# Two added waits on TensorE's own products in the expert stage of an attention and expert layer

## What is computed

```
x = L0_attn_x                                   # 4 x 1024 x 256
xn = _layernorm(x)
# attention of each batch of 1024 tokens
p = softmax(einsum('bqd,bkd->bqk', q, k) / 16); z = einsum('bqk,bkd->bqd', p, v)
# experts: 16 experts, the best 2 of each token, hidden width 128
h = silu(xt @ We_gate[e].T) * (xt @ We_up[e].T)
y = sum over the 2 chosen e of score * (h @ We_down[e].T)
# a shared expert of hidden width 512, gated by a sigmoid
return x + z + y + sigmoid(xt @ Wsg.T) * shared
```

## Time and profile before

| | |
|---|---|
| median of three executions | 540.95 us (540.4 to 541.15) |
| span of the profiled execution, first to last instruction | 535.7 us |
| median less span | 5.2 us |
| granted TensorE clock, mean | 0.997 of full speed |
| PE busy, share of the span | 96% (516.2 us) |
| VectorE, ScalarE, GpSimd busy | 75%, 52%, 32% |

### The profile page before, as it was taken

The page is one execution under the profiler, slowest core; times in us unless marked ns, Lnnn a source line. Parts: engine busy times, 40 slices in busy tenths (PEclk is TensorE's granted clock), DMA queues, the critical chain, the costliest instruction groups (busy, mean ns, idle before and its releaser), DMA issues.

```text
span 535.7 us, 10052 instructions
## 1 busy us (share of the span) xinstructions
PE 516.2 (96%) x3475; PEld 470.2 (88%) x3475; DVE 401.4 (75%) x842; ACT 277.7 (52%) x466; POOL 173.2 (32%) x161
## 2 busy tenths in 40 slices
PE   8999999999999699998999999999999999999997
PEld 6898898898888689988889989898989898989897
DVE  6997466898985466666666458998796969697986
ACT  4696865246652354444444545654453627272751
POOL 0001121101027565566662170517060424224302
PEclk9999999999999899999999999999999999999999
DMA  8926275122025355774456550443034111212112
GB/s 308 411 111 256 90 284 216 32 59 60 31 79 165 121 159 158 226 246 159 162 157 146 167 179 12 113 163 89 20 111 166 59 60 50 61 39 81 39 40 80
DMA packets 29840, 69.16 MB, mean 129 GB/s; under 512 B 4992, under 2 KB 9472, under 8 KB 28768
## 3 DMA queue, kind: packets, MB, share of 16 engines
q1 hardware_dynamic: 22496, 49.68, 25.8%
q0 software_dynamic: 6864, 18.75, 13.1%
q10 hardware_dynamic: 432, 0.09, 0.1%
HBM read 41.24 MB, written 27.26 MB: 128 GB/s over the span
## 4 chain that ended last, share of the span: by engine, by line
PE 81%; DVE 8%; issue 3%; another core or an unknown queue 3%; ACT 2%; DMA 1%; POOL 0%; SPq 0%; POOLq 0%; DVEq 0%; ACTq 0%
PE ps L771 52%; PE ps L981 9%; PE ps L777 6%; PE ps L911 6%; PE ps L1013 4%; PE ps L866 1%; ACT blk_xT L1105 1%; DVE blk_xT L1311 1%; PE ps L928 1%; DVE pT L1311 1%; DMA rows_y<-ytab,slot 1%; DVE probs_f L1646 1%; PE ps L875 1%; DVE place_hot L1497 1%
## 5 line engine op out<-in xcount | busy, mean ns | idle before, releaser
L758 POOL DMA_INDIRECT rows_y<-ytab,slot x64 | 77.6, 1213 | 148.1 <-DVE acc L1661 131.7
L738 POOL DMA_INDIRECT blk_x<-rows,row x79 | 81.0, 1025 | 79.4 <-DVE row L1512 30.5
L771 PE MATMUL ps<-vv,pT 128*128 128x258 f32 x768 | 97.6, 284 | 0.0
L771 PEld LDWEIGHTS ps<-vv,pT 128*128 128x128 f32 x768 | 95.2, 189 | 1.0
L771 PE MATMUL ps<-xT,shared_w 128*128 128x512 f32 x384 | 92.7, 394 | 0.4 <-DVE sil L1389 0.3
L771 PEld LDWEIGHTS ps<-xT,shared_w 128*128 128x128 f32 x384 | 70.7, 188 | 15.5 <-issue 0.9
L771 PE MATMUL ps<-qT,xbT_hi 128*128 128x512 f32 x256 | 79.3, 391 | 0.0
L981 PE MATMUL ps<-expert_w,blk_xT 128*128 x474 | 66.9, 290 | 5.8 <-DVE blk_xT L1311 5.3
L981 PEld LDWEIGHTS ps<-expert_w,blk_xT 128*128 128x128 f32 x474 | 59.5, 191 | 8.4 <-issue 8.3
L771 PEld LDWEIGHTS ps<-qT,xbT_hi 128*128 128x128 f32 x256 | 47.0, 188 | 9.2
L1299 ACT ACTIVATE probs_f<-probs_f 128x1024 f32<-128x1024 f32 x32 | 33.5, 1048 | 35.4 <-DVE probs_f L1646 35.4
(11 more groups left out here) (166 smaller groups left out, 857.7 us busy)
## 6 DMA issues: line engine op xcount, KB each, us to landing
ytab<-blk_y SPq DMA_DIRECT2D x40, 256.0 KB
keys<-xT SPq DMA_DIRECT2D x8, 1024.0 KB, 6.1
stage_e<-in_experts SPq DMA_DIRECT2D x16, 384.0 KB, 3.1
rows<-xn SPq DMA_DIRECT2D x8, 512.0 KB, 3.5
xbT_hi<-keys SPq DMA_DIRECT2D x8, 512.0 KB
xbT_lo<-keys SPq DMA_DIRECT2D x8, 512.0 KB
out<-acc SPq DMA_DIRECT2D x32, 128.0 KB
acc<-in_x SPq DMA_DIRECT2D x7, 512.0 KB, 9.0
```

Source lines behind the costliest of these rows:

```text
L738: e.indirect_dma_start(out=blk_x[:, q, n, :], out_offset=None, in_=rows, in_offset=bass.IndirectOffsetOnAxis(ap=row[:, 2 * b + n:2 * b + n ...
L758: e.indirect_dma_start(out=rows_y[:, r, k, :], out_offset=None, in_=ytab, in_offset=bass.IndirectOffsetOnAxis(ap=slot[:, k, i:i + 1], axis=0),
L771: ins = e.matmul(dst, stationary(p, k), moving(q, k), start=(n == 0), stop=(n == total - 1))
```

## The change

Two steps of TensorE's program get their waits in another order and one wait more each.

In `blk_hidden` the wait for the gated values was first in the code, and is now behind the wait for the buffer. A wait follows for `blk_gu` at `2 * (b + 1) + 1`: the first block of pair `b + 1`, whose twelve products stand directly ahead in TensorE's stream. In `blk_turn` the bank's wait now comes first and the wait for the fetched rows second, and from pair 4 on a wait follows for `blk_downed` at `2 * (b - 4) + 1`: the first block of pair `b - 4`, whose six products stand directly ahead. No other engine's program changes, and nothing is moved past another instruction.

```diff
                 elif kind == "blk_turn":
                     b, q = a[0], a[0] % XR
+                    bank = turn_bank(("blk_turn", b))
                     e.wait_ge(blk_loaded[q], 16 * (2 * (b // XR) + used(b)))
-                    bank = turn_bank(("blk_turn", b))
+                    if b >= 4:
+                        e.wait_ge(blk_downed, 2 * (b - 4) + 1)
                     turn(ps[:, bank, :], [blk_x[:, q, n, k * P:(k + 1) * P] for n in range(used(b)) for k in range(KD)],
                          blk_turned)
...
                     b, r = a[0], a[0] % 2
-                    e.wait_ge(blk_hidden, b + 1)
                     if b >= 2:
                         e.wait_ge(blk_hT_lo, b - 1)
                     else:
                         e.wait_ge(shared_added, 4 * NCH)
+                    e.wait_ge(blk_hidden, b + 1)
+                    if b + 1 < PAIRS:
+                        e.wait_ge(blk_gu, 2 * (b + 1) + 1)
                     turn(ps[:, 4 + r, :], [blk_h[:, r, n, :] for n in range(used(b))], blk_h_turned)
```

## The result

The changed kernel takes 554.25 us (median of four executions, 553.22 to 554.86), the kernel before beside it 540.68. The ratio is 1.025, interval 1.024 to 1.027: 2.5% slower. The forecast said slower, but only by 4.3 us, and its range ended at 550. The profiled execution has a span of 551.1 us, 15.4 more than before.

What follows compares the result with a forecast made beforehand. TensorE, busy 81% of the span, was taken as the bound, with late signals stalling the middle stretch. Eight gaps outside it (1.8 us) plus 2.5 us gave 4.3 us: 540.95 becomes 545.2 us, range 534 to 550.

Steps and rivals of the forecast that it cites:

- The reordered waits: Waits reordered in TensorE's `blk_hidden` and `blk_turn`: 0.01 us, only where `blk_hidden` or the rows are late; taken as 0.
- the wait for `blk_gu`: Ahead of the transposes of `blk_h`, 39 times: 0.40 us to spare, so 0 unless the signal is later than that.
- The gap of a TENSOR_LOAD: Ahead of every second product group, behind the `blk_downed` wait: 0.22 us each, 18 times, 4.0 us if all show.
- the term of the middle stretch: Experts' stage, 223.6 to 289.4 us: TensorE loses 1.2 us a cycle, 0.95 already lost; ten cycles cost 2.5 us.
- The 5.2 us that I took as lying around the span: Time outside the profiled span of 535.7 us, kept unchanged to go from span to measured time.
- 75 waits of 50 to 100 ns: 39 `blk_gu` and 36 `blk_downed` semaphore reads: 4 to 7 us if none were hidden; left out of the sum.
- The large loss: Rival: TensorE drains on late signals at both waits, gathers' credit comes later: 11.5 + 1.8 us, 554 us; chance 0.03.
- held-back signals come in time: Rival: without the queue's lead TensorE's signals arrive in time; 5.5 us less, 535.4, or 531.5 with hidden gaps; chance 0.29.
- it does nothing: Rival: gaps fall on stalls and signals are no later for TensorE than ScalarE; within 1 us, 541; chance 0.14.
- late signals belong to the profiler: Rival: tracing makes signals late, timed steps take 2.80 us, nothing is absorbed, 18 gaps cost 4.0: 544.9 us; chance 0.14.

Runs made afterwards that it cites:

- e3: The changed kernel without both new waits, only the old waits reordered, on the chip where the kernel before takes 518.2 us: 518.43 us, ratio 1.000.
- e1: The changed kernel without its `blk_downed` waits (`blk_gu` alone), on the chip where the kernel before takes 518.2 us: 518.15 us, ratio 1.000.
- e8: The changed kernel with the wait for `blk_gu` alone, run again on a chip where signals are late: 539.1 us, ratio 1.002.
- e2: The changed kernel without its `blk_gu` waits (`blk_downed` alone), on the chip where the kernel before takes 518.2 us: 522.42 us, ratio 1.007.
- e6: The kernel before with SyncE's plain loads of fixed rows (wrong tokens) in place of GpSimd's gathers: 527.97 us, ratio 0.981.
- e12: The changed kernel with SyncE's plain loads of fixed rows (wrong tokens) in place of GpSimd's gathers: 532.96 us, ratio 0.991 to the kernel before.
- e9: The changed kernel with the wait for `blk_downed` alone, run again on a chip where signals are late: 549.49 us, ratio 1.021.
- e10: The changed kernel with both waits, but the one for `blk_downed` behind the four transposes of the turn of `blk_x`: 545.66 us, ratio 1.0125.
- e7: The kernel before with one more GpSimd wait, for `blk_gu`, ahead of a pair's second gather: 536.14 us, ratio 0.995.

## Why the prediction was wrong

**What held.** The reordered waits cost nothing where no signal is late (e3: 1.000), and the reordering together with the wait for `blk_gu` costs next to nothing, be signals in time or late (e1: 1.000, e8: 1.002). The gap of a TENSOR_LOAD is 0.22 us where nothing is late (e2), and 18 of them 4.0 us (4.2 in e2, 5.0 from e6 to e12). Between the gathers of the changed kernel it is 0.32. The late signals need the gathers (e6). The direction was right.

**The step that failed** is the term of the middle stretch: "TensorE then loses 1.0 - 0.04 + 0.22 = 1.2 us a cycle, of which 0.95 was lost already: 0.25 x 10 = 2.5 us". The lateness of 1.0 was near what showed (1.32 in e9), but subtracting the stall was wrong. I took that stall as slack of TensorE that a delay may use up, since it "ends by ScalarE and GpSimd". It is the surplus of a loop that runs through TensorE: GpSimd waits for `blk_turned`, and the next signals come late while its next four gathers run. Its round of 6.56 us bounds the stretch, not TensorE's 5.60. The wait ahead of the turn puts the turn (0.63 us), and a restart and a later second pair (0.26), inside that loop; nothing is there to absorb them, and the round grows by 0.89 us (0.86 on average, 0.72 with the one wait of e9). The sum had 0.25. And it grows in twelve of the 13 runs of four gathers, not in 10, in the first stretch too, where I had counted only TENSOR_LOADs: 10.3 us where the sum had 2.5. That it is the place of the wait and not its length that costs is shown by e8, where TensorE waits as well and loses 0.4 us, and by e10, where the same wait behind the turn leaves the round at 6.60.

Two smaller points. The 5.2 us that I took as lying around the span are about 2 us in every run that lists both; the forecast is a difference and does not change by it. And 75 waits of 50 to 100 ns are 3.8 to 7.5 us, not 4 to 7, in a sentence that the sum leaves out.

**The rivals.** The large loss (0.03) named 554 us and the later credit of the gathers, which is the cause; but it priced it by the lateness of the signals at both waits, and e9 shows that one wait makes all of it. Its number was right partly by luck, its chance far too low. That held-back signals come in time (0.29) is excluded: TensorE waited up to 1.4 us for them in e9. That it does nothing is excluded by the measured 1.025. That late signals belong to the profiler (0.14) is not settled in full: the Trainium skill (NOTIFIC — the notification-queue block, 7.1 Overflow) says that the block that writes trace records can push back, and every execution here is recorded. But on the chip with 518.2 us the same recording goes with no late signal, and the signals are on time without gathers (e6), so recording alone does not make them late.

**What stays open.** How the gathers make the signals late: some come while the fourth gather runs (262.54), the last only 0.8 us behind its end, and in e3 none is late. Why the chip with 518.2 us shows none; it ran in one session, so that the chip and something else in that session are not told apart. Whether a gap between gathers would help: e7 made none. Why e10 still loses 7.6 us though its rounds of four are short again; its many rounds of two are argued from the trace.

## What to carry to other kernels

A stall on the busiest engine is slack for a delay only if the delayed instruction is not part of the loop that ends the stall. Before subtracting a stall from a new delay, follow one round: which engine's wait starts the next piece of work elsewhere, and where the instruction that grants it stands. Here a row of the idle engine (GpSimd, 1.61 us ahead of every fourth gather) and its round of 6.56 us told the bound. A wait ahead of the granting instruction made each round 0.7 to 0.9 us longer; the same wait behind it left the round of four as it was, and a wait at another place (`blk_gu`) cost 0.4 us in all.

## What the runs showed of the hardware

TensorE's semaphore signals can come late while GpSimd's indirect gathers follow each other. The last of them came mostly about 0.8 us behind the end of the fourth gather, whether ScalarE waited (its copy 0.73 to 0.85 us behind in the kernel before) or TensorE itself (its turn 0.78 to 1.07 in the changed one); others came while the third or fourth gather ran, 0.45 us late in the kernel before (the copy at 256.32) and 0.86 us later than due in the changed one (262.54). With plain loads from SyncE in place of the gathers none was late. It did not show everywhere: the same kernel took 518.2 us on one chip and 538 to 541 us on the others, and on the first a variant of it (e3) ran more than 40 gathers in a row with no signal late.
